# A fused four-layer kernel: the three phase orders of its engines become one order over the whole program

## The chip, the cores and the metric

The kernel runs on one core of a Trainium2 chip. A core has five engines that run side by side and meet at semaphores: PE (TensorE, matrix products and transpositions), DVE (VectorE), ACT (ScalarE), POOL (GpSimd) and SP, which here only issues transfers. The metric is the device time of one launch in microseconds (us); lower is better. The kernel before takes 1239.77 us, the median of three runs (1237.17 to 1240.85).

## The reference

Four layers are applied, one behind the other, to 32 samples of 128 tokens by 128 features; each sample has a condition vector of 128 numbers. All numbers are float32.

```
mod = silu(c) @ W_mod + b_mod                                  # layer 0: 16 heads of 64
x = x + g_msa * attention(modulate(layernorm(x)), W_qkv, W_out)
x = x + g_mlp * ff(modulate(layernorm(x)))                     # ff: 128 -> 512 -> gelu -> 128
x = x + proj(attention(film(rmsnorm(x))))                      # layer 1: one head of 128
x = x + mlp(film(rmsnorm(x)))
x = x + gate1 * attention(modulate(layernorm(x)))              # layer 2: 16 heads of 8
x = x + gate2 * ff(modulate(layernorm(x)))
self = [x, q] @ W_self.T + b_self                              # layer 3: graph attention
for d in range(2):                                             # on A = adj, then adj transposed
    cond, vb = A.sum(-1), A @ w_bias + b_bias                  # adj: 128 x 128 x 11 int32 a sample
    out += gat(self, first 20 tokens as keys, masked by cond > 0, bias vb)
x = x + relu(self + out)
```

## The kernel before

**Groups and streams.** The 32 samples are handled in 8 groups of 4 (`G`, `NG`), so that a tile is 128 partitions by 512 columns. The work of a group is cut into four streams, each a fixed list of steps: the front (layer 0's attention in 8 rounds of two heads, `front_steps`, 77 steps, or 74 for the last group), the middle (layer 0's feed-forward and layer 1, `mid_steps`), the back (layer 2, `back_steps`; it also turns the int32 labels of layer 3 into sums, in 12 pieces, one step of every third) and the end (layer 3, `end_steps`). Below, "front 7" is the front stream of group 7, "end 5" the end stream of group 5, and so on. Names of steps that the text uses: in the front `qk` and `v` (projections), `S` (scores), `T` and `T'` (transposition of the probabilities of one head each), `a` (attention times values), `o` (output projection), `stat`, `unit`, `turn` (norm of the next group: statistics, scaling, transposition and modulation) and `y` (residual); in the back `stat`, `unit`, `turn` of norm 4, then `kq2`, `v2`; in the end `adj` (label sums), `sum3`, `self3`, `qk3` and `u3`, which is thirteen units.

**Four streams at a time.** A stream of a group follows that of the same kind of the group before, and its own group's stream before it. So front g+3, middle g+2, back g+1 and end g run side by side. Every engine has a program of its own, and it is in order: `weave` (line 419) takes one letter after the other from a string and lets the stream of that letter emit its next step on this engine. The strings are tables (`ORDERS`, lines 190 to 244), one for each of PE, DVE, ACT and POOL, in three phases: `head` (fronts 0 to 2, middles 0 and 1, back 0), `steady` (one order of 170 steps, emitted four times, for fronts 3 to 6, middles 2 to 5, backs 1 to 4 and ends 0 to 3) and `tail` (the rest). `order_pairs` (line 256) lists which step must stand before which, and each table is held against it. All loops are Python's, so the built program is straight code.

**PSUM banks.** Results of PE go to 8 banks. `Phase` (line 303) walks PE's order and deals to each result the bank that was released longest ago in that order. It starts anew at each phase. A PE step waits until the bank it writes was emptied by its last reader (`empty`) and until its own inputs are there (`drained`).

**Transfers.** SP's sequence is written out by hand (lines 680 to 712): the input of the next norm (`x_norm`), the residual (`x_res`), the labels of the next group (`adj0`, `adj1`), and the store of a finished group, each behind a wait for the tile's last reader.

## Time and profile before

| | |
|---|---|
| median of three runs | 1239.77 us |
| the profiled execution, whole | 1240.78 us |
| its span, first to last instruction | 1239.0 us |
| PE busy / share | 1110.0 us / 90% |
| DVE busy / share | 879.8 us / 71% |
| ACT busy / share | 772.8 us / 62% |
| POOL busy / share | 434.2 us / 35% |
| mean granted clock of PE | 0.946 |
| instructions | 24134 |

PE is the busiest engine. Steps can be found in the trace, since every step issues a fixed number of instructions of a known line and the engine is in order; so the times of steps below are start times of rows. The four `steady` turns lie between about 308 and 845 us. A granted clock of 1.00 is 2.4 GHz and one of 0.50 is 1.2 GHz. The program before ends with the store of group 7.

### The profile page before, as it was taken

What the parts mean: (1) busy time and instruction counts of PE and PEld (TensorE: products, weight loads), DVE (VectorE), ACT (ScalarE), POOL (GpSimd) and SP (SyncE); (2) the same over time, 40 slices, a digit from 0 to 9 for tenths busy, and PEclk for the clock granted to TensorE, in tenths of its full rate; (3) what the DMA queues carried; (4) which work ended last, traced back from release to release, by engine and by line L of the source; (5) the groups of instructions that cost most, each with busy time, mean ns of one, the idle gap of its engine ahead of it and who ended that gap; (6) DMA issues with size and microseconds to landing.
All of it is one profiled execution on the core that took longest, in us unless ns stands there. A gap on an engine that the chain in (4) does not pass through costs nothing.

```text
span 1239.0 us, 24134 instructions
## 1 busy us (share of the span) xinstructions
PE 1110.0 (90%) x8411; PEld 748.2 (60%) x8411; DVE 879.8 (71%) x2510; ACT 772.8 (62%) x2888; POOL 434.2 (35%) x599
## 2 busy tenths in 40 slices
PE   5889989989999999999999999998989977879865
PEld 4655755665567656775667656765666545646533
DVE  3456656775888688987799688877786478656655
ACT  1646557874688648873787468863866546726622
POOL 1322323332254333541445225432453234214313
PEclk9999999999999999999999999998979998886695
DMA  8000000001000100000000100010000100010000
GB/s 246 2 10 10 10 1 1 10 10 31 1 10 10 31 10 10 1 28 20 9 3 11 39 1 10 2 31 9 10 2 1 38 1 1 1 38 1 1 9 9
DMA packets 21822, 20.98 MB, mean 17 GB/s; under 512 B 1143, under 2 KB 20296, under 8 KB 21448
## 3 DMA queue, kind: packets, MB, share of 16 engines
q1 hardware_dynamic: 18536, 15.26, 4.4%
q10 hardware_dynamic: 3168, 4.19, 1.1%
q8 instruction: 69, 1.13, 0.4%
q14 instruction: 49, 0.40, 0.1%
HBM read 17.35 MB, written 2.10 MB: 16 GB/s over the span
## 4 chain that ended last, share of the span: by engine, by line
PE 63%; DVE 24%; ACT 7%; POOL 3%; issue 2%; DMA 1%; POOLq 0%; DVEq 0%; ACTq 0%
PE bank L1017 9%; PE bank L1036 7%; PE bank L1024 6%; PE bank L1142 5%; PE bank L1041 4%; PE bank L1074 4%; PE bank L1084 4%; PE bank L1150 3%; PE bank L1059 3%; PE bank L1068 3%; PE bank L1011 3%; PE bank L1232 2%; ACT prob_space L947 2%; PE bank L1221 2%; ACT fprobs L883 2%
## 5 line engine op out<-in xcount | busy, mean ns | idle before, releaser
L771 POOL TENSOR_TENSOR fprobs<-fprobs,frinv 128x512 f32<-128x512 f32 x128 | 132.4, 1039 | 282.5 <-DVE frinv L1327 282.2
L883 ACT ACTIVATE fprobs<-bank,fnegmax 128x128 f32<-128x128 f32 x512 | 180.8, 385 | 63.3 <-DVE fnegmax L1322 63.2
L947 ACT ACTIVATE prob_space<-bank,negmax 128x128 f32<-128x128 f32 x512 | 180.7, 380 | 22.2 <-DVE negmax L1451 21.9
L1017 PE MATMUL bank<-fhT,w_qkv 128*128 128x512 f32 x256 | 124.2, 607 | 1.6 <-DVE edge L1521 0.8
L883 ACT ACTIVATION_READ_ACCUMULATOR fprobs<-bank,fnegmax 128x1 f32 x512 | 115.6, 226 | 0.0
L947 ACT ACTIVATION_READ_ACCUMULATOR prob_space<-bank,negmax 128x1 f32 x512 | 113.4, 222 | 0.0
L1322 DVE TENSOR_REDUCE fnegmax<-bank 128x4 f32<-128x512 f32 x128 | 82.1, 682 | 43.7 <-PE bank L1059 43.7
L744 POOL TENSOR_TENSOR rstd<-veps,half 128x4 f32<-128x4 f32 x40 | 40.8, 1019 | 204.5 <-DVE veps L1284 184.3
L1451 DVE TENSOR_REDUCE negmax<-bank 128x4 f32<-128x512 f32 x128 | 82.3, 684 | 31.8 <-PE bank L1142 31.6
L889 ACT ACTIVATE fprobsT<-bank 128x512 f32<-128x512 f32 x128 | 74.4, 602 | 48.6 <-PE bank L1068 48.6
L1150 PE MATMUL bank<-ident,prob_space 128*128 128x128 f32 x512 | 86.3, 300 | 7.6 <-ACT prob_space L947 4.1
L953 ACT ACTIVATE prob_space<-bank 128x512 f32<-128x512 f32 x128 | 76.1, 609 | 26.8 <-PE bank L1150 26.7
L1068 PE MATMUL bank<-ident,fprobs 128*128 128x128 f32 x512 | 75.4, 278 | 17.3 <-POOL fprobs L771 14.8
L1068 PEld LDWEIGHTS bank<-ident,fprobs 128*128 128x128 f32 x512 | 58.7, 142 | 50.2 <-POOL fprobs L771 25.3
L894 ACT ACTIVATE fk<-bank 128x512 f32<-128x512 f32 x64 | 38.6, 603 | 73.2 <-PE bank L1017 72.7
L1142 PE MATMUL bank<-km,qk 32*128 32x256 f32 x512 | 80.9, 437 | 1.0 <-issue 0.8
L1150 PEld LDWEIGHTS bank<-ident,prob_space 128*128 128x128 f32 x512 | 63.4, 153 | 27.9 <-issue 19.8
L1059 PE MATMUL bank<-fk,fq 64*128 64x128 f32 x1024 | 75.2, 287 | 2.2 <-DVE fq L1332 1.6
L1024 PEld LDWEIGHTS bank<-w_qkv,fhT 128*128 128x128 f32 x512 | 64.9, 191 | 18.8 <-issue 16.5
L1059 PEld LDWEIGHTS bank<-fk,fq 64*128 64x128 f32 x1024 | 63.2, 189 | 19.0 <-issue 16.7
L1084 PE MATMUL bank<-fattnT,w_out 128*128 128x512 f32 x128 | 68.5, 617 | 5.6 <-DVE fattnT L1344 5.6
L801 POOL TENSOR_TENSOR adjw<-adjf,labels 80x176 f32<-80x176 f32 (+1 forms) x96 | 54.5, 568 | 52.3 <-ACT adjf L942 52.3
(193 smaller groups left out, 2499.0 us busy)
## 6 DMA issues: line engine op xcount, KB each, us to landing
adj<-in_mask_BxSxSx_ik SPq DMA_DIRECT2D x8, 440.0 KB
adj<-in_mask_BxSxSx_ik SPq DMA_DIRECT2D x32, 110.0 KB
x_norm<-in_x SPq DMA_DIRECT2D x8, 256.0 KB, 2.9
x_res<-in_x SPq DMA_DIRECT2D x8, 256.0 KB, 2.9
out<-x_out SPq DMA_DIRECT2D x8, 256.0 KB, 2.3
w_qkv<-in_L_cond_W_qkv ACTq DMA_DIRECT2D x1, 1536.0 KB, 7.0
prob_space<-in_w_mod SPq DMA_DIRECT2D x1, 1024.0 KB
w_up<-in_w_up ACTq DMA_DIRECT2D x1, 768.0 KB, 12.7
```

The lines of the kernel that those rows point to most:

```text
L771: pool.tensor_tensor(p, p, wide(frinv[:, u, :], D), ALU.mult).then_inc(fnormed.sem, 1)
L883: ins = act.activation(fprobs[:, u % NP, b, :], P.bank(("S", u))[:, tok(b)], ACT.Exp, bias=fnegmax[:, u, b:b + 1], accum_out=frsum[:, u, b ...
L947: ins = act.activation(probs[:, u % NP, i, :], P.bank(("A", u))[:, tok(i)], ACT.Exp, bias=negmax[:, u, i:i + 1], accum_out=rsum[:, u, i:i ...
L1017: ins = pe.matmul(P.bank(result)[:, :], w, a, start=(i == 0), stop=(i == len(terms) - 1))
L1024: ins = pe.matmul(P.bank(result)[:, tok(b)], a[:, tok(b)], w, start=(i == 0), stop=(i == len(terms) - 1))
L1036: pe.matmul(P.bank(result)[:, :], w_up[:, l, tok(c)], part.hT[:, :], start=True, stop=True).then_inc(P.full_sem(result), 1)
L1059: ins = pe.matmul(P.bank(("S", 2 * c + r))[:, tok(b)], fq[rows, c % 2, tok(b)], fk[rows, c % 2, tok(b)], start=True, stop=True)
L1068: ins = pe.transpose(P.bank(("T", u))[:, tok(b)], fprobs[:, u % NP, b, :], ident[:, :])
L1084: ins = pe.matmul(P.bank("o0")[:, :], w_out[:, c, :], fattnT[:, c % 2, :], start=(c == 0), stop=(c == C0 - 1))
L1142: ins = pe.matmul(P.bank(("A", u))[:, tok(2 * n, 2)], qk[strip(u), 0, tok(b)], flat(km[strip(u), b % 2, 2 * n:2 * n + 2, :]), start=True, ...
L1150: ins = pe.transpose(P.bank(("T", u))[:, tok(i)], probs[:, u % NP, i, :], ident[:, :])
L1451: dve.tensor_reduce(negmax[:, u, :], P.bank(("A", u))[:, :].rearrange("p (i k) -> p i k", i=HS), AX.X, ALU.max, negate=True).then_inc(max2 ...
```

## The change

The three phases go. There is one string for each engine over all 1357 steps, with a letter of its own for each stream of each group (fronts A to H, middles I to P, backs Q to X, ends a to h). `Plan` deals the banks once, over the whole of PE's order, in place of `Phase`. The pairs of `order_pairs` are written as a loop over the groups. Two waits are added that the phases had made superfluous: PE waits, before the first `qk` of a front, for the modulated input (`drained("ln0")`), and DVE waits, before the first piece of labels of a back, for its own `bias_ready` of the group before. SP no longer has its sequence written out: its loads and stores are emitted at steps of the streams, in DVE's order.

The strings are not a new arrangement from scratch. Each step's place in PE's order moves by 1.9 places in the mean (at most 17), in DVE's by 1.9 (19), in ACT's by 3.0 (30), in POOL's by 4.1 (49), of 1357. The sequence in which SP issues its transfers is the same, instruction by instruction, and so is the sequence of ACT's 38 table loads, two of exp and gelu in turn.

The diff, cut. Of the strings of letters one line of each side stands:

```diff
@@ -155,19 +155,10 @@
 
 
 
-
-STEPS = {"F": front_steps(), "M": mid_steps(), "B": back_steps(), "E": end_steps(), "A": front_steps(), "Q": front_steps(),
-         "U": mid_steps(), "L": front_steps(False), "N": mid_steps(), "C": back_steps(), "D": back_steps(), "G": end_steps(),
-         "H": end_steps(), "I": end_steps()}
-STEP_NS = {"F": {"qk": 1720, "T": 440, "T'": 440, "S": 1000, "v": 900, "E": 300, "a": 1000, "I": 100, "stat": 300, "unit": 300, "turn": 450,
-                 "o": 860, "y": 500},
...
+for _g in range(NG):
+    STEPS.update({FRONTS[_g]: front_steps(_g + 1 < NG), MIDS[_g]: mid_steps(), BACKS[_g]: back_steps(), ENDS[_g]: end_steps()})
 
 
 NPIECES = 12
...
 ORDERS = {
-    "head": {
+    "all": {
         "PE": (
...
-            "AAAAAAAAAAAAAAAAAAAAAAAAAAAAAAAAAAAAAAAAAAAAAAAAAAAAAAAAAAAAAAAAAAAAAAAAAAAQAQUUQQQQUQQQQQQQQQUQUQQU"
...
+            "IBBBIIBBBBBBBBBIBIBIIBIBIBBBBBBBIBBIBBBIIIBBBBBBBBBBBBIBBBIBIBBIBBIBBCCBBBBCCBBCBCQCCBCCQJJCCCCCJCQC"
...
@@ -261,27 +256,34 @@
 
         pairs.append(((a, len(STEPS[a]) - 1), (b, 0)))
 
-    for f, m in (("Q", "U"), ("F", "M"), ("L", "M")):
-
-        pairs.append((step_at(m, "back", 0), step_at(f, "y")))
-    for a, f in (("A", "Q"), ("Q", "F")):
-
-        pairs += [(step_at(a, x, C0 - 1), step_at(f, y)) for x, y in (("S", "S"), ("I", "E"), ("T'", "T"), ("v", "v"), ("a", "a"), ("o", "o"))]
-        pairs += [(step_at(a, x), step_at(f, y)) for x, y in (("turn", "qk"), ("y", "stat"))]
+    for g in range(NG):
+        f, m, b, e = FRONTS[g], MIDS[g], BACKS[g], ENDS[g]
+
+        follow(f, m)
+        follow(m, b)
+        follow(b, e)
+        if g + 1 == NG:
+            break
+        f2, m2, b2, e2 = FRONTS[g + 1], MIDS[g + 1], BACKS[g + 1], ENDS[g + 1]
+
+        follow(m, m2)
+        follow(b, b2)
+        follow(e, e2)
+
+        pairs.append((step_at(m, "back", 0), step_at(f2, "y")))
+
+        pairs += [(step_at(f, x, C0 - 1), step_at(f2, y)) for x, y in (("S", "S"), ("I", "E"), ("T'", "T"), ("v", "v"), ("a", "a"), ("o", "o"))]
+        pairs += [(step_at(f, x), step_at(f2, y)) for x, y in (("turn", "qk"),)]
+        pairs.append((step_at(f, "y"), step_at(f2, "stat") if g + 2 < NG else step_at(f2, "o", C0 - 1)))
         for c in range(2):
-            pairs += [(step_at(a, "S", C0 - 2 + c), step_at(f, "qk", c)), (step_at(a, "T'", C0 - 2 + c), step_at(f, "S", c)),
-                      (step_at(a, "a", C0 - 2 + c), step_at(f, "T", c)), (step_at(a, "o", C0 - 2 + c), step_at(f, "a", c))]
-        pairs += [(step_at(a, "a", C0 - 4 + c), step_at(f, "v", c)) for c in range(4)]
-
-    for a, b in ("AU", "UM", "QM", "UB", "LN", "MN", "MC", "BC", "ND", "CD", "EG", "BG", "GH", "CH", "HI", "DI"):
-        follow(a, b)
-    for b, m in ("BM", "CN"):
-
-        pairs.append((step_at(b, "y2"), step_at(m, "down", (1, 1))))
-    for e, b in ("EB", "GC", "HD"):
-
-        pairs.append((step_at(e, "adj"), (b, EDGE_EVERY * 3)))
-        pairs.append((step_at(e, "u3", NU3 + 4), step_at(b, "down", (2, 1))))
+            pairs += [(step_at(f, "S", C0 - 2 + c), step_at(f2, "qk", c)), (step_at(f, "T'", C0 - 2 + c), step_at(f2, "S", c)),
+                      (step_at(f, "a", C0 - 2 + c), step_at(f2, "T", c)), (step_at(f, "o", C0 - 2 + c), step_at(f2, "a", c))]
+        pairs += [(step_at(f, "a", C0 - 4 + c), step_at(f2, "v", c)) for c in range(4)]
+
+        pairs.append((step_at(b, "y2"), step_at(m2, "down", (1, 1))))
+
+        pairs.append((step_at(e, "adj"), (b2, EDGE_EVERY * 3)))
+        pairs.append((step_at(e, "u3", NU3 + 4), step_at(b2, "down", (2, 1))))
     return pairs
 
 
...
@@ -300,57 +302,51 @@
         assert not order_faults(_order), (_name, order_faults(_order))
 
 
-class Phase:
-
-
-
-    def __init__(self, banks, orders, turns=1, prefer=range(8)):
+class Plan:
+
+
+
+    def __init__(self, banks, orders, prefer):
         self.banks, self.orders = banks, orders
         order = orders["PE"]
-        self.base = list(banks.dealt)
         starts = {x: [p for p, y in enumerate(order) if y == x] for x in set(order)}
         ends = {(x, r): starts[x][i] for x in starts for i, s in enumerate(STEPS[x]) for r in s.ends}
         free_from = {b: i - 100 for i, b in enumerate(prefer)}
-        for _ in range(2 if turns > 1 else 1):
-            self.at, self.per = {}, [0] * 8
-            went = dict.fromkeys(starts, 0)
-            for p, x in enumerate(order):
-                for r in STEPS[x][went[x]].begins:
-                    b = min(free_from, key=lambda b: free_from[b])
-                    assert free_from[b] < p, (p, x, r)
-                    free_from[b] = ends[x, r]
-                    self.at[x, r] = (b, self.per[b])
-                    self.per[b] += 1
-                went[x] += 1
-            free_from = {b: p - 1000 for b, p in free_from.items()}
-        for b in range(8):
-            banks.dealt[b] += turns * self.per[b]
-
-    def view(self, letter, turn):
-        return View(self, letter, turn)
+        self.at, dealt = {}, [0] * 8
+        went = dict.fromkeys(starts, 0)
+        for p, x in enumerate(order):
+            for r in STEPS[x][went[x]].begins:
+                b = min(free_from, key=lambda b: free_from[b])
+                assert free_from[b] < p, (p, x, r)
...
@@ -642,6 +632,14 @@
         def strip(u):
             return slice(32 * (u % S4), 32 * (u % S4) + 32)
 
+        def run(name, prologue, front, mid, back, last):
+            prologue()
+            streams = {}
+            for letters, stream in ((FRONTS, front), (MIDS, mid), (BACKS, back), (ENDS, last)):
+                streams.update({letter: stream(plan.view(letter), g) for g, letter in enumerate(letters)})
+
+            weave(plan.orders["DVE" if name == "SP" else name], streams)
+
...
-            for g in range(2):
-                sp.wait_ge(*fz_ready.nth(g, 0))
-                load_norm(g + 1)
-            for g, mid_letter in enumerate("UM"):
-                sp.wait_ge(*head.view(mid_letter, 0).drained("z0"))
-                load_res(g + 1)
-                sp.wait_ge(*fz_ready.nth(g + 2, 0))
-                load_norm(g + 3)
-            sp.wait_ge(*adj_summed.nth(0, NPIECES - 1))
-            load_edges(1)
-
-            def steady_loads(it, norm):
-                sp.wait_ge(*steady.view("M", it).drained("z0"))
-                load_res(it + 3)
-                if norm is not None:
-                    sp.wait_ge(*fz_ready.nth(it + 4, 0))
-                    load_norm(norm)
-                sp.wait_ge(*adj_summed.nth(it + 1, NPIECES - 1))
-                load_edges(it + 2)
-                store(steady.view("E", it), it)
-
-            for it in range(NG - 4):
-                steady_loads(it, it + 5 if it + 5 < NG else None)
-            sp.wait_ge(*tail.view("M", 0).drained("z0"))
-            load_res(NG - 1)
-            sp.wait_ge(*adj_summed.nth(NG - 3, NPIECES - 1))
-            load_edges(NG - 2)
-            store(tail.view("E", 0), NG - 4)
-            sp.wait_ge(*adj_summed.nth(NG - 2, NPIECES - 1))
-            load_edges(NG - 1)
-            for i, letter in enumerate("GHI"):
-                store(tail.view(letter, 0), NG - 3 + i)
+            sp.wait_ge(*fz_ready.nth(0, 0))
+            load_norm(1)
+
+            def front(P, g):
+                for what, _, _, _ in STEPS[P.letter]:
+                    if what == "unit" and g + 2 < NG:
+                        sp.wait_ge(*fz_ready.nth(g + 1, 0))
+                        load_norm(g + 2)
+                    yield
+
+            def mid(P, g):
+                for what, _, _, _ in STEPS[P.letter]:
+                    if what == "back" and g + 1 < NG:
+                        sp.wait_ge(*P.drained("z0"))
+                        load_res(g + 1)
+                    yield
+
+            def back(P, g):
+                for i in range(len(STEPS[P.letter])):
+                    if i == EDGE_LAST and g + 1 < NG:
+                        sp.wait_ge(*adj_summed.nth(g, NPIECES - 1))
+                        load_edges(g + 1)
+                    yield
+
+            def last(P, g):
+                for what, _, _, _ in STEPS[P.letter]:
+                    if what == "y3":
+                        store(P, g)
+                    yield
+
+            run("SP", lambda: None, front, mid, back, last)
...
-
-        def run(name, prologue, front, mid, back, last):
-            prologue()
-            weave(head.orders[name], A=front(head.view("A", 0), 0), Q=front(head.view("Q", 0), 1), F=front(head.view("F", 0), 2),
-                  U=mid(head.view("U", 0), 0), M=mid(head.view("M", 0), 1), B=back(head.view("B", 0), 0))
-            for it in range(NG - 4):
-                weave(steady.orders[name], F=front(steady.view("F", it), it + 3), M=mid(steady.view("M", it), it + 2),
-                      B=back(steady.view("B", it), it + 1), E=last(steady.view("E", it), it))
-            weave(tail.orders[name], L=front(tail.view("L", 0), NG - 1), M=mid(tail.view("M", 0), NG - 2),
-                  N=mid(tail.view("N", 0), NG - 1), B=back(tail.view("B", 0), NG - 3), C=back(tail.view("C", 0), NG - 2),
-                  D=back(tail.view("D", 0), NG - 1), E=last(tail.view("E", 0), NG - 4), G=last(tail.view("G", 0), NG - 3),
-                  H=last(tail.view("H", 0), NG - 2), I=last(tail.view("I", 0), NG - 1))
 
         @block.gpsimd
         def _(pool):
@@ -1045,12 +1030,15 @@
             def front(P, g):
                 for what, c, _, _ in STEPS[P.letter]:
                     if what == "qk":
+                        if c == 0 and g:
+
+                            pe.wait_ge(*plan.view(FRONTS[g - 1]).drained("ln0"))
                         linear(P, f"q_{c}", [(w_qkv[:, tok(c)], fhT[:, :])])
                         linear(P, f"k_{c}", [(w_qkv[:, tok(C0 + c)], fhT[:, :])])
                     elif what == "v":
...
@@ -1440,6 +1428,9 @@
                     if not 0 <= p < NPIECES:
                         return
                     d, e0, n = PIECES[p]
+                    if p == 0 and g:
+
+                        dve.wait_ge(*bias_ready.nth(g - 1, 0))
                     dst = edge1[:, :, e0:e0 + n] if d else edge0[:, :, 0, e0:e0 + n]
                     dve.wait_ge(*adjw_ready.nth(g, p))
                     _, labels, weighted = edge_views(p)
@@ -1495,7 +1486,7 @@
                         add(P, "y2", x, x1)
                     elif what == "down" and k == (2, 1):
                         dve.wait_ge(*P.drained("xt"))
-                        if P.phase is not head:
+                        if g:
 
                             dve.wait_ge(*rel_ready.nth(g - 1, 1))
                         dve.wait_ge(*P.full("g2"))
```

Three places show what the strings do. The names are those of the profile: `fattnT` is what `o` reads, `fz` the gated result that `y` transposes, `x3T` the input of layer 3, `z` and `mz` the scaled norms of the back and of the middle, `hT` and `mhT` the modulated ones, `edge` the label sums. Line numbers after the change are lower by 8 to 15.

PE before, at the end of front 7, from the last but one `o` on:

```order
L1084 MATMUL bank<-fattnT,w_out 128x512
L1074 MATMUL bank<-fprobsT,fv 64x128 x8
L1084 MATMUL bank<-fattnT,w_out 128x512
L1011 MATMUL bank<-ident,fz 128x128 x4
L1182 MATMUL bank<-ident,edge 128x80 x2
L1017 MATMUL bank<-x3T,ones 128x512
L1011 MATMUL bank<-ident,z 128x128 x4
L1017 MATMUL bank<-x3T,w 128x512
L1017 MATMUL bank<-q,w 128x512
L1017 MATMUL bank<-hT,w_l 128x512 x2
```

PE after, the same place:

```order
L1072 MATMUL bank<-fattnT,w_out 128x512
L1062 MATMUL bank<-fprobsT,fv 64x128 x8
L1002 MATMUL bank<-x3T,ones 128x512
L1072 MATMUL bank<-fattnT,w_out 128x512
L996 MATMUL bank<-ident,z 128x128 x4
L1002 MATMUL bank<-x3T,w 128x512
L1002 MATMUL bank<-q,w 128x512
L996 MATMUL bank<-ident,fz 128x128 x4
L1002 MATMUL bank<-hT,w_l 128x512 x2
```

The transposition of back 6 (`ident,z`) and the first products of end 5 (`x3T`) now stand ahead of front 7's last step (`ident,fz`), and the label sums (`edge`) further up.

DVE before, at the same place, from the copy behind the last but one `a` on:

```order
L1344 COPY fattnT<-bank 128x512
L1356 COPY fmod<-mod 128x4
L1344 COPY fattnT<-bank 128x512
L1302 TENSOR_SCALAR fz<-bank,col,fmod 128x128 x4
L1364 TENSOR_TENSOR x_res<-bank,x_res 128x512
L1398 COPY gmod<-mod 128x64
L1459 TENSOR_SCALAR biasg<-gmod,col 128x4
L1272 BN_STATS stats<-x 128x6 x4
L1275 MEMSET held 128x1
L1277 BN_AGGR mv<-stats 128x2 x4
L1284 TENSOR_SCALAR veps<-mv 128x4
L1518 COPY gcond<-condT 128x4
```

DVE after:

```order
L1332 COPY fattnT<-bank 128x512
L1386 COPY gmod<-mod 128x64
L1450 TENSOR_SCALAR biasg<-gmod,col 128x4
L1260 BN_STATS stats<-x 128x6 x4
L1263 MEMSET held 128x1
L1265 BN_AGGR mv<-stats 128x2 x4
L1272 TENSOR_SCALAR veps<-mv 128x4
L1344 COPY fmod<-mod 128x4
L1332 COPY fattnT<-bank 128x512
L1528 TENSOR_SCALAR q<-bank,gcond 128x128 x4
L1280 TENSOR_SCALAR z<-x,mv,rstd 128x128 x4
L1290 TENSOR_SCALAR fz<-bank,col,fmod 128x128 x4
```

The statistics of back 6 stand between two copies of front 7, where DVE waited for PE, and its scaling (`z`) ahead of `fz`.

PE before, around norm 2 of middle 7 (`mz`), with bank numbers and waits:

```order
L1232 MATMUL bank6<-kbd,q3 128x80 [waits bank7_free,bank6_free]
L1232 MATMUL bank7<-kbd,q3 128x80
...
L1150 MATMUL bank4<-ident,prob_space 128x128 [waits bank4_free,bank1_free]
L1150 MATMUL bank4<-ident,prob_space 128x128 x3
L1150 MATMUL bank3<-ident,prob_space 128x128 [waits bank3_free,bank2_free]
L1150 MATMUL bank3<-ident,prob_space 128x128 x3
L1011 MATMUL bank7<-ident,mz 128x128 [waits bank7_free,mid_z_ready]
```

PE after:

```order
L1130 MATMUL bank5<-km,qk 128x256 [waits bank6_free,bank5_free,km_ready]
L1130 MATMUL bank6<-km,qk 128x256
...
L1138 MATMUL bank7<-ident,prob_space 128x128 [waits bank7_free,bank5_free]
L1138 MATMUL bank7<-ident,prob_space 128x128 x3
L1138 MATMUL bank1<-ident,prob_space 128x128 [waits bank1_free,bank6_free]
L1138 MATMUL bank1<-ident,prob_space 128x128 x3
L996 MATMUL bank6<-ident,mz 128x128 [waits bank6_free,mid_z_ready]
```

The transposition stands at the same place, but its bank was last held by scores of back 6, which ACT reads, and no longer by scores of end 5, which DVE reads at unit 3.

## Rows read from the trace of the kernel before

**Rows 1.** The page: span, busy time of each engine with its share.
```profile
span 1239.0 us, 24134 instructions
PE 1110.0 (90%) x8411; PEld 748.2 (60%) x8411; DVE 879.8 (71%) x2510; ACT 772.8 (62%) x2888; POOL 434.2 (35%) x599
```
**Rows 2.** Busy time by stretch: length, PE, PEld, DVE, ACT, POOL, clock, DMA.
```profile
165.00:308.00 143.00, 128.97 (x956) 85.65 (x954) 92.05 (x281) 92.87 (x358) 41.17 (x48) 0.99 0.04 11
845.00:920.00 75.00, 66.75 (x437) 43.72 (x437) 58.95 (x161) 49.45 (x192) 32.86 (x48) 0.86 0.02 5
1032.00:1083.00 51.00, 42.66 (x361) 30.80 (x361) 36.29 (x101) 34.67 (x126) 20.21 (x29) 0.80 0.01 1
1083.00:1239.00 156.00, 116.60 (x742) 75.88 (x742) 91.32 (x249) 64.47 (x215) 48.05 (x80) 0.73 0.04 12
```
**Rows 3.** Busy time in the third steady turn, same columns.
```profile
569.70:704.30 134.60, 129.68 (x1054) 87.96 (x1050) 110.05 (x313) 94.99 (x360) 53.43 (x73) 1.00 0.05 14
```
**Rows 4.** PE's waits in that turn: for whom, us, times, longest.
```profile
PE bank L1017 <- DVE edge L1521: 1.2, 1, 1.2
PE bank L1011 <- DVE z L1292: 0.8, 1, 0.8
```
**Rows 5.** Busy time in stretches of half clock, columns of rows 2.
```profile
903.40:917.10 13.70, 12.46 (x83) 9.57 (x84) 10.96 (x27) 6.25 (x25) 9.13 (x11) 0.50 0.00 1
1033.10:1043.30 10.20, 9.37 (x36) 5.68 (x37) 8.40 (x19) 4.50 (x21) 6.34 (x8) 0.50 0.00 0
1121.90:1162.90 41.00, 39.05 (x251) 27.68 (x247) 24.79 (x61) 28.85 (x127) 14.52 (x25) 0.50 0.01 1
```
**Rows 6.** Timeline around 990 to 1003: start, us, instruction, [idle before, releaser].
```profile
989.40 0.69 DVE L1344 COPY fattnT<-bank 128x512 f32<-128x512 f32 x1 [2.18 <-PE bank L1074]
991.38 1.37 DVE L1302 TENSOR_SCALAR fz<-bank,col,fmod 128x128 f32<-128x128 f32 x4 [1.29 <-PE bank L1084]
997.75 1.11 DVE L1292 TENSOR_SCALAR z<-x,mv,rstd 128x128 f32<-128x128 f32 x4
998.77 1.12 DVE L1537 TENSOR_SCALAR q<-bank,gcond 128x128 f32<-128x128 f32 x4
998.91 1.09 PE L1011 MATMUL bank<-ident,z 128*128 128x128 f32 x4 [4.41 <-DVE z L1292]
1002.96 1.45 PE L1017 MATMUL bank<-hT,w_l 128*128 128x512 f32 x3
```
**Rows 7.** Timeline from 851 to 857.
```profile
852.71 1.28 DVE L1322 TENSOR_REDUCE fnegmax<-bank 128x4 f32<-128x512 f32 x2
856.35 3.78 PE L1017 MATMUL bank<-hT,w_l 128*128 128x512 f32 x4 [2.84 <-DVE hT L1297]
```
**Rows 8.** Timeline from 1031 to 1034.
```profile
1031.31 0.86 DVE L1290 TENSOR_SCALAR mz<-mx,rstd 128x128 f32<-128x128 f32 x4
1033.35 0.43 DVE L1570 TENSOR_TENSOR p<-bank,keep 128x320 f32<-128x320 f32 x1
1033.93 1.09 PE L1011 MATMUL bank<-ident,mz 128*128 128x128 f32 x4 [3.93 <-DVE p L1570]
```
**Rows 9.** Timeline of PE from 79 to 98.
```profile
79.93 0.66 PE L1068 MATMUL bank<-ident,fprobs 128*128 128x128 f32 x4 [1.56 <-POOL fprobs L771]
88.57 1.88 PE L1017 MATMUL bank<-fhT,w_qkv 128*128 128x512 f32 x4
90.76 1.06 PE L1024 MATMUL bank<-w_qkv,fhT 128*128 128x128 f32 x8
97.54 0.85 PE L1011 MATMUL bank<-ident,mz 128*128 128x128 f32 x4 [1.82 <-DVE mz L1292]
```
**Rows 10.** PE's waits from 165 to 308, columns of rows 4.
```profile
PE bank L1084 <- DVE fattnT L1344: 2.4, 3, 0.8
PE bank L1068 <- ACT fk L894: 1.5, 1, 1.5
```
**Rows 11.** All waits of the span: DVE's only one for a load.
```profile
DVE stats L1272 <- DMA x_norm<-in_x: 8.6, 1, 8.6
```

156 lines of the change are left out of this document (77 added, 79 removed).

## The prediction

> **What bounds the kernel.** I read the page first: of a span of 1239.0 us PE is busy 1110.0, DVE 879.8 [rows 1]. The change adds and removes no work, so what can move is PE's waiting (129.0 us) and its clock. Then busy time by stretch [rows 2], to see where the waits lie: 14.0 us of 143 from 165 to 308, 8.3 of 75 from 845 to 920, 8.3 of 51 from 1032 to 1083, 39.4 of 156 behind 1083. A steady turn instead lasts 134.6 us and has 129.7 of PE in it at full clock [rows 3]: 4.9 us of waits, four times. So the turns are near PE's work, and the stretches in which the phases meet are looser: at the turn's rate (3.7%) the three named first would hold 9.8 us of waits and not 30.6. Last the granted clock: 0.86, 0.80 and 0.73 in the stretches from 845 on, 1.00 in the turn [rows 2, 3]. In half-clock stretches PE is busy nearly throughout (12.5 of 13.7 us, 9.4 of 10.2, 39.1 of 41.0 [rows 5]); of such busy time half is what the clock costs, since two projections take 1.88 us at full clock and 3.78 at half [rows 7, 9].
>
> **The change, place by place.** Times are of the profiled execution: its span 1239.0 and 1.8 around it, 1240.8, which is 1.0 above the median of 1239.8; I take that 1.0 off in the end.
>
> A. End of front 7. From the copy behind the last `a` (989.40) to back 6's `kq2` (1002.96) pass 13.6 us [rows 6]. DVE waits 1.29 us for `o`, gates `fz`, and only then takes the statistics of back 6, the label tiles and `z`, for which PE waits 4.41. After, statistics and labels stand ahead of the copy, in DVE's former waits (2.18 in rows 6), and from the copy on DVE has copy 0.69, `q` 1.12, `z` 1.11, `fz` 1.37 and `hT`, which has the shape of `fz`, 1.37: 5.7 in a row. On PE `q` needs `sum3` first, so that `z` is done at about 3.3; behind it stand the transposition (0.66), `self3`'s two products (1.88) and `y` (0.66), so `kq2` starts at about 6.5, when `hT` is there too. Gain 13.6 - 6.5 = 7.1, full clock assumed.
>
> B. Start of back 5. PE waits 2.84 us for `hT` before `kq2` [rows 7]. After, DVE modulates directly behind front 7's row maxima, and `adj` and `v` (1.06 [rows 9]) stand ahead of `kq2` on PE. Behind `z` DVE has a residual add of 0.7, the maxima 1.28 and the modulation 1.37, 3.3 together; PE has a transposition 0.66, `adj` 0.3 and `v` 1.1, so about 1.2 of waiting is left: gain 1.6 here and 0.8 just ahead, 2.4. `kq2` ran at half clock; that costs 1.9 by its 3.78, and some 3.0 with what follows it. I take half: 3.9 in all, between 1 and 5.4.
>
> C. 893 to 917. PE waits for POOL and DVE at end 4's units (8.3 us in 845 to 920, less the 3.7 of B, 4.6), and the clock falls at 903.4 for 13.7 us [rows 2, 5]. The new order puts one transposition (0.66) more ahead of the waiting unit, little else. Between 0 and 4.6 + 6.2; I take 2.0, near the 0.66 and a part of the clock.
>
> D. Middle 7's norm 2. `mz` is ready at 1032.17, but PE starts at 1033.93, when DVE has read unit 3's scores out of bank 7 [rows 8]. After, the bank is one that ACT empties earlier: 1.8 of the 3.9 go. Then the clock falls for 10.2 us, with PE busy 9.4 [rows 5]; half of it, 4.7, would come back if it didn't, and I take half of that, 2.3. Further down `u3` and transpositions move ahead of waits of 1 to 2 us, 1.0 taken. 5.1, between 1 and 16 (all 8.3 of the stretch and more clock).
>
> E. End of front 0. Front 1's `qk` and `v`, 1.88 + 1.06, move ahead of `T`, which waits 1.56 and then 0.7 [rows 9]. But the same 1.88 lay between `o` and `y` before, and covered the gate (1.37): that wait opens. What remains is 0.9, and `qk` ahead of the `mz` transposition covers 0.4 more of its 1.82. With half of the half-clock stretch behind it 2.1, between 0.5 and 3.
>
> F. 165 to 308. `qk`, `S` and `v` now stand before both `o` of front 1 (its share of the 2.4 us is 1.6) and two steps before the `T'` that waited 1.5 [rows 10]; with `y` and the clock behind the second 4.0 of 14.0, between 0 and 8.
>
> S. The four turns. `kq2` waits 1.2 us for a bank that holds the label sums, and the `z` transposition before it 0.8 [rows 4]. After, middle g+2's scaling (1.1) is no longer ahead of `z` on DVE, in all turns. Of 8.2 us I take 3.0. The bounds are -8 and +33 (below).
>
> G. Behind 1083. PE's order moves by two places at most here, and the waits are those of one chain: 0, between -6 and +6.
>
> H. What the moves open elsewhere. Nearly every step moves by a place or two. A turn, one tuned order, has seven waits of 0.7 in the mean (4.9 in all). I put two more of them into each 134.6 us from 77 to 1083: 7.5 x 1.4 = +10.5. It may be 0, or twice that.
>
> Sum: 7.1 + 3.9 + 2.0 + 5.1 + 2.1 + 4.0 + 3.0 = 27.2, less 10.5, is 16.7. 1240.8 - 16.7 - 1.0 = 1223.1: **1223 us**.
>
> The other edits cost nothing. PE's new wait for the modulated input stands five or more of PE's working steps behind the transposition that feeds it, against one modulation of 1.4 us. DVE's is for a result of its own, earlier in its order. SP issues the same transfers in the same order. The one load that any engine waits for is the first [rows 11], which doesn't move; were SP's loads later by some us, they would still be hidden.
>
> **A rule against the sum.** The sum holds that a turn can win its waits and no more, since PE's busy time is a floor: in the third turn PE is busy 129.7 of 134.6 us [rows 3]. The Trainium skill, page "Perfetto Trace Analysis", section "Identifying the Most-Contended Engine", says that matmul busy time is no good measure of nearness to the roofline, and the weight loads' is. By it the turn would not be bound by PE: weight loads are busy 88.0 us of it, DVE 110.1 [rows 3]. The turn could then fall until DVE binds, by up to 24.5 us, four times 98: about 1125. Against it in rows: between waits PE's instructions stand end to start, and a reordering changes none of them; so far the trace does not bear the rule out.
>
> **Rivals.**
> 1. The clock stays up. If the waits at 903 and 1033 shrink, the half-clock stretches behind them may go whole: 6.2 more in C, 2.4 in D and about 4 in the two further dips to 1071, and H is 3 rather than 10.5. 1223 - 12.6 - 7.5 = 1203. For it: each dip sits behind a wait of over 1.5 us. Against: waits of 1.2 and 1.8 in one stretch may do as well.
> 2. Given back. The named waits go, but the end is one chain from end 6 to the store, in which the clock is half for 41 us [rows 5] anyway. If that stretch grows by the 25 us that are at full clock around it, PE's work there takes 12 more: 1223 + 12, and a few us of H: 1236 to 1243.
> 3. Slower, through banks in the turns. The new plan deals other banks in each turn, and a step can meet one whose reader is late, as bank 7 did for 1.8 us [rows 8]. If the turns wait like 165 to 308 does (9.8% in place of 3.7%), each is 8.2 longer, 33 in four, against 24.2 won elsewhere: 1240 + 9 = 1249. It decides from about 6 us a turn on, three or four such meetings. For it: before's turn was one order, tuned and repeated; now four different ones. Against: the distance from a bank's release to its next use, in PE's order, is the same before and after (three steps or more, seven mostly).
> 4. The rule above, 1125.
> That the change does nothing is half true: SP's sequence is unchanged, so all of the effect must come from the four strings.
>
> **How the numbers follow.** Forecast (1212 to 1235) 0.52; rival 1 (1195 to 1212) 0.17; rival 2 0.15; rival 3 0.15; rival 4 0.01. About 0.3%, 3.7 us, is what a measurement can tell from no change. Faster: 0.52 + 0.17 + 0.01 = 0.70; same, rival 2, 0.15; slower 0.15. The range reaches into rival 1 and over most of rival 2: 1206 to 1241. The forecast's own is 1212 to 1235.
>
> **What would show it.** A: from the copy behind the last `a` of front 7 to `kq2` of back 6 under 8 us. B: the wait before back 5's `kq2` near 1.2. D: the transposition of middle 7's `mz` within 0.3 us of `mz`. E: a new wait of 1.4 before front 0's `y`, none of 1.56 at its last `T`. S: turns of about 134. H: waits that before doesn't have, some 10 us. PE's busy time in the turns unchanged. I am wrong if a turn is over 137 or under 130, if the clock from 845 to 1083 is 1.00 throughout (rival 1), or if the part behind back 7's start grows by over 6 us (rival 2).

## The result and the profile after

The changed kernel takes **1183.87 us** (median of 4 runs, 1181.46 to 1187.39) against 1240.31 of before beside it (1237.17 to 1244.25): ratio 0.9546, interval 0.9509 to 0.9582. Faster by 56 us; 1223 was forecast, with a range from 1206.

The page of after, answering to [rows 1]; the execution took 1181.46 us.

```profile
span 1179.7 us, 24111 instructions
PE 1085.0 (92%) x8411; PEld 734.9 (62%) x8411; DVE 881.7 (75%) x2510; ACT 770.1 (65%) x2888; POOL 435.8 (37%) x599
```

Two things moved. PE waits 94.7 us (1179.7 - 1085.0) and not 129.0: 34.3 less. And PE's busy time, with the same 8411 matmuls, is 25.0 shorter: less of it at half clock. To see where, I cut after at the PE steps at which the prediction's windows begin and end. A cut falls behind the same number of steps, not always behind the same steps. First the stretches of before that no group has shown (columns of rows 2):

```profile
0.00:165.00 165.00, 139.27 (x969) 95.98 (x971) 87.95 (x252) 85.69 (x321) 45.02 (x54) 0.99 0.17 52
308.00:845.00 537.00, 516.91 (x4179) 351.08 (x4178) 438.81 (x1244) 379.56 (x1440) 212.75 (x291) 1.00 0.05 14
920.00:1032.00 112.00, 98.80 (x777) 65.07 (x777) 74.45 (x227) 66.07 (x243) 34.18 (x49) 0.98 0.04 12
```

and all seven of after, with its third turn last, answering to [rows 2, 3]:

```profile
0.00:163.40 163.40, 141.43 (x965) 97.45 (x966) 88.56 (x253) 86.70 (x327) 45.83 (x55) 0.99 0.18 53
163.40:292.90 129.50, 127.01 (x977) 85.40 (x975) 93.52 (x292) 92.76 (x351) 41.25 (x49) 1.00 0.04 12
292.90:822.10 529.20, 520.15 (x4175) 354.91 (x4176) 439.47 (x1238) 378.05 (x1440) 214.07 (x291) 0.99 0.05 14
822.10:889.60 67.50, 60.09 (x416) 39.66 (x416) 56.56 (x149) 48.63 (x191) 29.47 (x45) 0.92 0.02 5
889.60:993.90 104.30, 97.30 (x787) 65.37 (x789) 78.29 (x236) 66.75 (x246) 36.73 (x52) 1.00 0.04 12
993.90:1035.60 41.70, 33.88 (x363) 24.64 (x362) 36.46 (x104) 33.00 (x122) 21.52 (x29) 1.00 0.01 2
1035.60:1179.70 144.10, 105.14 (x739) 67.43 (x736) 88.81 (x242) 64.21 (x216) 46.91 (x79) 0.79 0.05 13
550.90:681.40 130.50, 128.70 (x1047) 88.76 (x1046) 109.26 (x314) 95.22 (x361) 54.22 (x73) 1.00 0.05 14
```

Length less PE is the waiting. Side by side, in us:

| stretch of before | length | waits | PE busy | forecast of the length |
|---|---|---|---|---|
| 0-165 | -1.6 | 25.7 to 22.0 | +2.2 | E -2.1 |
| 165-308 | -13.5 | 14.0 to 2.5 | -2.0 | F -4.0 |
| 308-845 (turns) | -7.8 | 20.1 to 9.1 | +3.2 | S -3.0, most of H +10.5 |
| 845-920 | -7.5 | 8.3 to 7.4 | -6.7 | B, C -5.9 |
| 920-1032 | -7.7 | 13.2 to 7.0 | -1.5 | A -7.1 |
| 1032-1083 | -9.3 | 8.3 to 7.8 | -8.8 | D -5.1 |
| behind 1083 | -11.9 | 39.4 to 39.0 | -11.5 | G 0 |

Down to the end of the turns the gain is waits (26.3 of 34.3), in the last phase it is mostly clock (28.4 less PE busy behind 845 of before). Two rows need a second look. In 0-165 PE is 2.2 us busier: the profiled execution of after ran its first projections at half speed, that of before did not, and neither did that of `s2_head` (experiment 2), which has the same new order there. The first four products in before, after and `s2_head`, in this order:

```profile
22.81 1.98 PE L1017 MATMUL bank<-fhT,w_qkv 128*128 128x512 f32 x4 [0.56 <-DVE fhT L1297]
```
```profile
22.63 3.78 PE L1002 MATMUL bank<-fhT,w_qkv 128*128 128x512 f32 x4 [0.55 <-DVE fhT L1285]
```
```profile
22.58 1.98 PE L1002 MATMUL bank<-fhT,w_qkv 128*128 128x512 f32 x4 [0.56 <-DVE fhT L1285]
```

`s2_head` takes 160.6 us for this stretch, so the order gained 4.4 here and not 1.6. And in 845-920 after has 416 matmuls for before's 437. Time at half clock went from about 20.5 us to 10.2, worth some 4.5; about 2 us of the 7.5 are work that only lies on the other side of a cut, so B, C gave about 5.

The places that the prediction worked out came as it said. Timeline of PE (with one row of DVE in it) where it answers to [rows 6 to 9]:

```profile
93.52 1.11 PE L996 MATMUL bank<-ident,fz 128*128 128x128 f32 x4 [1.54 <-DVE fz L1290]
102.69 0.66 PE L996 MATMUL bank<-ident,mz 128*128 128x128 f32 x4 [1.44 <-DVE mz L1280]
...
825.13 1.13 PE L1002 MATMUL bank<-hT,w_l 128*128 128x512 f32 x2 [1.38 <-DVE hT L1285]
...
957.05 0.69 DVE L1332 COPY fattnT<-bank 128x512 f32<-128x512 f32 x1 [0.42 <-PE bank L1062]
960.30 0.66 PE L996 MATMUL bank<-ident,z 128*128 128x128 f32 x4 [1.38 <-DVE z L1280]
962.95 1.89 PE L1002 MATMUL bank<-hT,w_l 128*128 128x512 f32 x4
...
993.04 0.66 PE L996 MATMUL bank<-ident,mz 128*128 128x128 f32 x4 [1.19 <-DVE mz L1278]
```

B: 1.38 us of waiting before back 5's `kq2`, where 2.84 were and 1.2 was forecast. A: from the copy to `kq2` 5.9 us (962.95 - 957.05), where 13.6 were and 6.5 was forecast. D: PE takes `mz` at once, not after the reader of bank 7. E: the wait for the gate has opened (1.54; forecast 1.4). The waits from 163.4 to 292.9 answer to [rows 10]; the two largest:

```profile
PE bank L1056 <- POOL fprobs L756: 1.1, 2, 0.6
PE bank L996 <- DVE mz L1280: 0.3, 1, 0.3
```

### The profile page after: what moved, and what is told of

It is laid out like the page before. It is cut to its first block, busy times and chain, and to the rows that moved or that the text cites. A ratio compares the mean times of both kernels' runs of the same rounds, so it can differ in the third digit from the quotient of the medians.

```text
span 1179.7 us, 24111 instructions
## 1 busy us (share of the span) xinstructions
PE 1085.0 (92%) x8411; PEld 734.9 (62%) x8411; DVE 881.7 (75%) x2510; ACT 770.1 (65%) x2888; POOL 435.8 (37%) x599
## 4 chain that ended last, share of the span: by engine, by line
PE 68%; DVE 19%; ACT 5%; POOL 4%; issue 3%; DMA 1%; POOLq 0%; DVEq 0%; ACTq 0%
PE bank L1002 11%; PE bank L1021 7%; PE bank L1009 7%; PE bank L1026 5%; PE bank L1047 5%; PE bank L1072 5%; PE bank L1062 5%; PE bank L1056 4%; PE bank L1130 4%; PE bank L1138 3%; PE bank L996 3%; PE bank L1148 2%; PE bank L1220 2%; PE bank L1209 2%; ACT prob_space L932 2%
## 5 line engine op out<-in xcount | busy, mean ns | idle before, releaser
L1138 PE MATMUL bank<-ident,prob_space 128*128 128x128 f32 x512 | 78.6, 287 | 6.0 <-ACT prob_space L932 5.6
L1130 PE MATMUL bank<-km,qk 32*128 32x256 f32 x512 | 75.6, 422 | 3.5 <-POOL km L793 2.2
L1138 PEld LDWEIGHTS bank<-ident,prob_space 128*128 128x128 f32 x512 | 60.6, 147 | 27.3 <-issue 17.6
L838 POOL TENSOR_TENSOR p<-p,rinv 128x320 f32<-128x320 f32 x64 | 47.3, 740 | 75.8 <-DVE rinv L1548 75.8
## 6 DMA issues: line engine op xcount, KB each, us to landing
w_up<-in_w_up ACTq DMA_DIRECT2D x1, 768.0 KB, 13.2
```

The costliest lines, as they stand in the source:

```text
L1130: ins = pe.matmul(P.bank(("A", u))[:, tok(2 * n, 2)], qk[strip(u), 0, tok(b)], flat(km[strip(u), b % 2, 2 * n:2 * n + 2, :]), start=True, ...
L1138: ins = pe.transpose(P.bank(("T", u))[:, tok(i)], probs[:, u % NP, i, :], ident[:, :])
```

## Experiments

All were timed beside before, whose median was 1241.43 in the first four, 1242.66 in the next four, 1241.32 and 1240.86 in the last two sets. Most cut before's and after's strings at a step and join them, in the form of the changed kernel (one string, letters A to X and a to h). Of such an edit one line of a string stands; the others differ likewise.

**1. The form alone.** `s1_one_plan`: before's phases laid end to end in one string, one plan of banks, SP's transfers emitted from the steps. Cut from the changed kernel:

```diff
...
-            "AAAAAAAAAAAAAAAAAAAAAAAAAAAAAAAAAAAAAAAAAAAAAAAAAAAAAAAAAAAAAAAAAAABBAAAAAAAAAIBIBBBBBIBBBBBBIBBIBBI"
+            "AAAAAAAAAAAAAAAAAAAAAAAAAAAAAAAAAAAAAAAAAAAAAAAAAAAAAAAAAAAAAAAAAAAAAAAAAAABABIIBBBBIBBBBBBBBBIBIBBI"
...
```

> The changed code, but the strings hold the old three phases' orders, laid end to end: one bank plan, the two added waits and SP's woven sequence without any move of a step. Theory 1 (all of the effect is in the moved steps): 1240, within 4 us of before. Theory 2 (a good part comes from dealing the banks without a fresh start at each phase): 1215 to 1230.

Measured 1242.79, ratio 1.0018 (0.9996 to 1.0039). The new form is worth nothing that can be told from zero; all lies in the strings.

**2. Phase by phase.** `s2_head`, `s3_turns`, `s4_tail`: the new strings in the first phase, in the four turns, or in the last phase only, against `s1_one_plan`. A line of each:

```diff
...
-            "AAAAAAAAAAAAAAAAAAAAAAAAAAAAAAAAAAAAAAAAAAAAAAAAAAAAAAAAAAAAAAAAAAAAAAAAAAABABIIBBBBIBBBBBBBBBIBIBBI"
+            "AAAAAAAAAAAAAAAAAAAAAAAAAAAAAAAAAAAAAAAAAAAAAAAAAAAAAAAAAAAAAAAAAAABBAAAAAAAAAIBIBBBBBIBBBBBBIBBIBBI"
...
```

> As one_plan, with the new order inside the first phase alone (fronts 0 to 2, middles 0 and 1, back 0), the rest in the old order. Theory 1 (the gain is local and additive; by the two traces PE has done the first 329 steps 17 us earlier): 1220 to 1226. Theory 2 (moving the head only shifts when later waits and clock falls come, so that little of it is kept): 1232 to 1240.

```diff
...
-            "GGUGUGdUdVVHeOHHHHHHHVeOOVHVHVeVVVOeVOeVVHVOVHHHVOHeHVHVHeOHVHOHVVVVeHHVVeeVOVOVeVVeOHVHeOHHHOHVHeHV"
+            "GNUGUUUdGVVHeOHHHHHHHVeOOVHVHVeVVVOeVOeVVHVOVHHHVOHeHVHVHeOHVHOHVVVVeHHVVeeVOVOVeVVeOHVHeOHHHOHVHeHV"
...
```

> As one_plan, with the new order inside the four steady turns alone. Theory 1: the two traces give 6.5 us here, with one fall of the clock in the new one: 1228 to 1236. Theory 2 (turns tuned one by one are no better than one repeated turn, and the 6.5 us come from what was before): 1238 to 1244.

```diff
...
-            "PfWWfPWWWPWWPPWWfPWWPWPfPWfWPWWPWWPfPWWWfWWfWWPWPffWWfWPWPWWWWPPWfWWWWgXXXgXXXgXXggXXXXgXXgXXXXXXXXg"
+            "WPWWWPPPWWfWWPWWfWPfWPWPfWWfWPPWPWWWPWWfWWPfWWPfPWWWfWfWPWPWWfWPWPWWWWgXXXgXXXXXgXgXXXXgXgXXXXgXXXXX"
...
```

> As one_plan, with the new order inside the last phase alone (front 7 on). Theory 1: the two traces give 35 us from PE step 1009 on: 1203 to 1209. Theory 2 (a part of the tail's gain is the clock, which falls by chance of when a wait comes, so it is not tied to these moves): 1212 to 1225.

Measured 1223.16 (ratio 0.9844, 0.9797 to 0.9891), 1233.56 (0.9936, 0.9918 to 0.9955) and 1211.96 (0.9773, 0.9741 to 0.9806): by these ratios 19, 8 and 28 us, 55 of the 56. The first two fall where their expectation had them. The third is 3 us above its theory 1 and just outside theory 2 (from 1212), so it decides between neither.

**3. The seams.** `s5_seams`: new strings, but no step ahead of one of an earlier phase. From it to the changed kernel:

```diff
...
-            "DaRDDKRKDDDaDKRRDRKRRKDDKRDDDRaDDKDDDRDDDaRKDDKDRRKDDDKDRDRDKDRDaRDDDaDRDKRDKDDDDRKaRDDRRaKRDRDaRRaE"
+            "DaRDDKRKDDDaDKRRDRKRRKDDKRDDDRaDDKDDDRDDDaRKDDKDRRKDDDKDRDRDKDRDaRDDDaDRDKRDKDDDDRKaRDDRRaKRDRDaRREa"
...
```

> The changed kernel with its new order inside every phase, but with the seams kept: no step of one phase stands ahead of a step of an earlier one (8 of PE's 1357 steps, 12 of VectorE's, 29 of ScalarE's and 70 of GpSimd's go back for that). Theory 1, the gain lies in the order inside the phases (the three phases alone gave 19, 8 and 28 us): 1184 to 1190 us. Theory 2, moving steps across the seams, which only one order for the whole program allows, gives a part of it: over 1192 us.

Measured 1187.54, ratio 0.9555 (0.9532 to 0.9577), 3.7 us above the changed kernel by the medians and 1 us by the ratios to before: theory 1. Moving steps across the seams, the thing that only one order allows, is a small part, and the intervals don't tell it from nothing.

**4. What in the last phase.** `s6_tail_a` has the new order to PE's step 1215 (about 1036 us of before), `s7_tail_b` from there on.

```diff
...
-            "PfWWfPWWWPWWPPWWfPWWPWPfPWfWPWWPWWPfPWWWfWWfWWPWPffWWfWPWPWWWWPPWfWWWWgXXXgXXXgXXggXXXXgXXgXXXXXXXXg"
+            "WPWWWPPPWWfWWPWWfPWWPWPfPWfWPWWPWWPfPWWWfWWfWWPWPffWWfWPWPWWWWPPWfWWWWgXXXgXXXgXXggXXXXgXXgXXXXXXXXg"
...
```

> The new order only from the start of the last phase to PE's step 1215 (before: 1009 to 1037 us, turns of fronts, middle and back 5 and 6), the order of before ahead of it and behind it. In the trace of before and after this stretch holds 11 us of the last phase's 28, and 17 lie behind it. Theory 1, what is gained behind step 1215 (TensorE 28 us less at half clock there) is a consequence of the waits closed ahead of it, and comes with them: 1212 to 1218 us, and the stretch behind 1215 is as long as in the changed kernel. Theory 2, it comes from the order behind 1215 itself: 1226 to 1233 us.

```diff
...
-            "PfWWfPWWWPWWPPWWfPWWPWPfPWfWPWWPWWPfPWWWfWWfWWPWPffWWfWPWPWWWWPPWfWWWWgXXXgXXXgXXggXXXXgXXgXXXXXXXXg"
+            "PfWWfPWWWPWWPPWWfWPfWPWPfWWfWPPWPWWWPWWfWWPfWWPfPWWWfWfWPWPWWfWPWPWWWWgXXXgXXXXXgXgXXXXgXgXXXXgXXXXX"
...
```

> The new order only from PE's step 1215 to the end, the order of before ahead of it. Theory 1 (the gain behind 1215 follows from what stands ahead of it): 1238 to 1242 us. Theory 2 (it comes from the order there): 1221 to 1228 us, with less time at half clock behind step 1215.

Measured 1224.01 (0.9856, 0.9819 to 0.9894) and 1229.91 (0.9900, 0.9878 to 0.9922): 18.6 and 12.8 us, which add up to the phase's 28 and 3 more, and neither theory's figure. Behind 1083 of before, the windows of `s1_one_plan`, `s6_tail_a` and `s7_tail_b` (columns of rows 2):

```profile
1083.90:1243.00 159.10, 120.96 (x742) 78.10 (x742) 91.03 (x249) 64.57 (x215) 48.12 (x80) 0.70 0.04 11
```
```profile
1064.60:1221.90 157.30, 119.15 (x742) 77.47 (x742) 91.50 (x249) 64.47 (x215) 47.87 (x80) 0.71 0.04 12
```
```profile
1079.60:1228.50 148.90, 110.25 (x739) 70.82 (x736) 88.13 (x242) 64.32 (x216) 46.90 (x79) 0.73 0.05 12
```

The waits are 38.1, 38.2 and 38.7. With the order of before there, the stretch takes 156.0 to 159.1 us and PE is busy 116.6 to 121.0 in six kernels (before, `s1_one_plan`, `s2_head`, `s6_tail_a`, `s12_bank`, `s13_place_a`), whatever stood ahead; with the new one 144.1 to 149.0 and 105.1 to 110.3 in the changed kernel, `s4_tail` and `s7_tail_b`. So it is the new order there, which I had priced at nothing, that lets the same work run with less of it at half clock. It explains 7 to 10 us of the 11.9: before's 156.0 is the shortest of the one kind and the changed kernel's 144.1 the shortest of the other, and the 4.8 us between that and `s7_tail_b` no run assigns. From there on up to 1083, from before's 1034, `s6_tail_a` gains some 3 us more in an unchanged order. (Two numbers of the expectations don't come out of the traces: behind step 1215 after has some 40 us less at half clock than before, not 28, and the gain in an unchanged order is this 3, not 4.4.)

**5. Whose order.** Behind step 1215 the new order on DVE, ACT and POOL but not on PE (`s18_tail_b_others`, edit against `s7_tail_b`), and in the first phase on PE and DVE but not on ACT and POOL (`s15_head_pe_dve`, against `s2_head`).

```diff
...
-            "PfWWfPWWWPWWPPWWfWPfWPWPfWWfWPPWPWWWPWWfWWPfWWPfPWWWfWfWPWPWWfWPWPWWWWgXXXgXXXXXgXgXXXXgXgXXXXgXXXXX"
+            "PfWWfPWWWPWWPPWWfPWWPWPfPWfWPWWPWWPfPWWWfWWfWWPWPffWWfWPWPWWWWPPWfWWWWgXXXgXXXgXXggXXXXgXXgXXXXXXXXg"
...
```

> Behind PE's step 1215 the new order on VectorE, ScalarE and GpSimd, and the order of before on PE; ahead of it the order of before. With PE's new order too it was 1229.9 us. Theory 1, PE's moves of one or two places there matter little and the other engines' order closes the waits: 1228 to 1233 us. Theory 2, PE's places do it: 1238 to 1243 us.

```diff
...
-            "CJCQCQCCCCCQQQCCCQCQQJQJCCCCCKRDaDDaRKKDDaaDRDRRDDaRDRRRKKRRDDDRDRDKDRKDRDRKaDDRDRDDKKDaDaRRRDDDDDDK"
+            "CQCCCQCCCCCJQCCCCQCQCCQQCCQQQKRDaDDaRKKDDaaDRDRRDDaRDRRRKKRRDDDRDRDKDRKDRDRKaDDRDRDDKKDaDaRRRDDDDDDK"
...
```

> The new order in the first phase on PE and VectorE alone; ScalarE and GpSimd keep the order of before there, and everything behind the phase is as before. The new order on all four gave 1223.2 us. Theory 1, PE's and VectorE's order closes the waits (my terms E and F, which I read from these two): 1222 to 1228 us. Theory 2, the larger moves of ScalarE and GpSimd (up to 23 places) do it, since half of the waits there are for exponentials and probabilities: 1232 to 1242 us.

Measured 1245.93 (1.0059, 1.0034 to 1.0085) and 1233.55 (0.9968, 0.9935 to 1.0000). Theory 2 in the second; the first is slower still than its theory 2 (1238 to 1243). Three engines in the new order and PE in the old one are 5 us slower than before, and 16 slower than with PE moved along; behind 1083 the stretch then takes 156.1 us, with 42.1 of waits, for `s7_tail_b`'s 148.9. With ACT and POOL left behind the head gives 7 of its 19 us. Where F lay, 143.0 us of before, the new order on all four engines takes 129.1 (`s2_head`) and on PE and DVE alone 141.2 (columns of rows 2):

```profile
160.60:289.70 129.10, 125.41 (x959) 84.03 (x959) 90.81 (x280) 91.48 (x351) 40.34 (x48) 1.00 0.04 12
```
```profile
164.70:305.90 141.20, 130.32 (x959) 86.04 (x959) 92.33 (x280) 92.61 (x351) 40.36 (x48) 0.98 0.04 11
```

The largest waits of the latter:

```profile
PE bank L1130 <- ACT mhid L898: 2.2, 1, 2.2
PE bank L1056 <- POOL fprobs L756: 1.9, 4, 0.6
PE bank L996 <- DVE fz L1290: 1.5, 1, 1.5
PE bank L1009 <- ACT mhid L893: 1.3, 1, 1.3
```

Two of the four are for ACT at work on `mhid`, in ACT's old order; in after neither is there. The waits for `fprobs`, the largest of before's, shrank with PE's and DVE's order alone:

```profile
PE bank L1068 <- POOL fprobs L771: 5.1, 6, 1.8
```

Other mixes of engines over the whole program were not tried.

**6. Moves at random.** Neighbouring steps of different streams exchanged, 45 pairs in before (`s10_rand45`), 30 in after (`s16_rand_after`): all of them on PE, and on each other engine the 17 to 29 that stood in the same order there.

```diff
...
-            "CCCQJCQJQQJJQQQQCCQCQQCJCQCCCCCCQJQQJCQQCQJQCCQQCCCCQJQQCJJCCJCQCQJQCJQCCCJQQJCCQQQJCQQCCQCQCJCCCCQJ"
+            "CCCQJCQJQQJJQQQQCCQCQQCJCQCCCCCCQJQQJCQQCQJQCCQQCCCQCJQQCJJCCJCQCQJQCJQCCCJQQJCCQQQJCQQCCQCQCJCCCCQJ"
...
```

> The order of before with 45 pairs of neighbouring steps of different streams exchanged, drawn at random, on all four engines alike; nothing is chosen by time. The prediction held that moved steps open new waits of their own (its term H, 10.5 us for 1000 moved steps, a tenth of which move here). Theory 1, moves at random open waits at about that rate or above it: 1242 to 1250 us. Theory 2, PE is so rarely short of input that neighbours can be exchanged freely: within 2 us of before, 1238 to 1242 us.

```diff
...
-            "bEEEEELEEESEbLSESLLESEEESSSEbELEESbLEEEEEEESLLSESbESSEbLELESEbSESESSFbTTMFFFcTMFcTTFFMFcFFTcTTMcMTTT"
+            "SEEEEELEEESEbLSESLLESEEESSSEbELEESbLEEEEEEESLLSESbESSEbLELESEbSESESSFbTTMFFFcTMFcTTFFMFcFFTcTTMcMTTT"
...
```

> The changed kernel with 30 pairs of neighbouring steps of different streams exchanged on all engines alike, drawn at random: 19 in the turns, 9 in the last phase. Theory 1, the turns stay within 1 us each and the last phase gets longer by some us, as 16 random exchanges in it did to the order of before (13.6 us): 1187 to 1197 us. Theory 2, the new order has so few waits that exchanges are free: 1182 to 1186 us.

Measured 1254.04 (1.0098, 1.0056 to 1.0139) and 1196.11 (0.9671, 0.9621 to 0.9722): 12 us lost each time. The second is within its theory 1, the first above it (1242 to 1250). Where: the turns of `s10_rand45` (28 of its exchanges, seven places four times over) and then 920 to 1083 of before.

```profile
307.50:842.80 535.30, 515.71 (x4179) 351.60 (x4176) 437.12 (x1244) 380.17 (x1440) 212.53 (x292) 1.00 0.05 14
919.20:1094.80 175.60, 143.75 (x1139) 95.96 (x1138) 111.95 (x328) 100.31 (x367) 54.77 (x79) 0.89 0.03 8
```

The turns take 535.3, not more than the 537.0 of before. The other stretch takes 175.6, where before's takes 163.0, with 31.9 us of waits for 21.5 and the clock at 0.89 for 0.93. In `s16_rand_after` 8.6 of the 13.0 us by which its profiled execution is longer than the changed kernel's lie behind the turns. So moves that nobody chose cost in the last phase, and there more than H: 45 exchanges, a tenth of the change's moved steps, took 12 us, and H charged 10.5 for all of them. In the turns they cost nothing. The change's moves opened fewer waits than they closed in every stretch: they are not of the kind that I had priced.

**7. One order for all turns.** `s11_turn4`: the changed kernel with the order of its fourth turn in the other three.

```diff
...
-            "cFFMTFFMFcTFMTMcTTcTFFFFMFcTMTFFTFTFTTGUGcUGGGGdGdUGNUUGNdUNUdUUNNdUdNUUUUGGNGdUUGGGNUGGGNGUGGNGUGUG"
+            "MFcTFFFFMcTFFFMMTFFcTcTTFFMcTFFMTFTTTGUcGFUGGGGdGdUGNUUGNdUNUdUUNNdUdNUUUUGGNGdUUGGGNUGGGNGUGGNGUGUG"
...
```

> The changed kernel with the order of its fourth turn in all four turns (its own turns last 133.0, 137.0, 130.6 and 131.9 us; the second holds 10.2 us at half clock). Theory 1, a stretch's time belongs to its order and is repeated with it: three turns of 131.8 in place of 133.0, 137.0 and 130.6, 5 us less than the changed kernel, 1177 to 1182 us. Theory 2, each turn's order is fitted to the banks and streams that its neighbours leave it: 1184 to 1192 us.

Measured 1185.78, ratio 0.9568 (0.9523 to 0.9613): no gain, theory 2. Two of its turns:

```profile
548.80:681.60 132.80, 130.41 (x1047) 88.05 (x1046) 111.08 (x312) 94.10 (x360) 54.00 (x73) 1.00 0.05 14
681.60:815.30 133.70, 131.31 (x1049) 88.43 (x1048) 111.08 (x312) 94.10 (x360) 54.00 (x73) 1.00 0.05 12
```

Each waits 2.4 us. The second is the fourth turn, whose string is unchanged; in the changed kernel it waits 1.4:

```profile
686.50:818.40 131.90, 130.47 (x1052) 88.48 (x1051) 111.19 (x316) 94.48 (x361) 54.02 (x73) 1.00 0.04 12
```

So what stands ahead of a turn changes its waits, here by 1 us. The gain that theory 1 expected did not come.

**8. Single places.** `s12_bank`: before with another bank for middle 7's norm 2. `s13_place_a`: before with the new order between steps 1150 and 1200 only. `s14_place_a_old`: after with before's order between 1160 and 1190.

```diff
...
+                if (x, r) == ("P", "ln2"):
+                    b = sorted(free_from, key=lambda b: free_from[b])[1]
...
```

> The order of before throughout, with one thing altered: the transposition of middle 7's norm 2 is dealt the second longest free bank in place of bank 7 (and what is dealt behind it follows). PE waits 1.8 us there for the reader of bank 7, and then the clock falls for 10.2 us. Theory 1 (my term D): the 1.8 go and half of what the clock costs there, 2.3, so 1236 to 1239 us. Theory 2, the wait alone goes: 1239 to 1241 us. Theory 3, the clock stays up behind it through the further stretches to 1163, 32 us of them at a cost of about 0.43 us each: under 1230 us.

```diff
...
-            "PfWWfPWWWPWWPPWWfPWWPWPfPWfWPWWPWWPfPWWWfWWfWWPWPffWWfWPWPWWWWPPWfWWWWgXXXgXXXgXXggXXXXgXXgXXXXXXXXg"
+            "WPWWfPWWWPWWPPWWfPWWPWPfPWfWPWWPWWPfPWWWfWWfWWPWPffWWfWPWPWWWWPPWfWWWWgXXXgXXXgXXggXXXXgXXgXXXXXXXXg"
...
```

> The new order only between PE's steps 1150 and 1200 (end of front 7, back 6's norm, kq2 and first end steps), the order of before elsewhere. Term A gave 7.1 us for this place; between before and after its two stretches (PE's steps 1111 to 1185) differ by 10.2 us. Theory 1, the place gives what it gives and nothing behind it: 1231 to 1235 us. Theory 2, with its waits gone the clock behind it stays up as in the run with the new order to step 1215 (4.4 us less in steps 1241 to 1270 with the same order): 1224 to 1229 us.

```diff
...
-            "HVHHeHOVHVHHHHVeVOHHOHVeHVVeHOVOHHHVHHOHHHVHVVOOeHHHHVVOVHHVHHHOHVVHHfWHHHHHfWHWfHWWfPWPWWPffPPWWWfP"
+            "HVHHeHOVHVHHHHVeVOHHOHVeHVVeHOVOHHHVHHOHHHVHVVOOeHHHHVVOVHHVHVVHHHOHHHHWHHHHHWffWfWWfPWPWPWffPPWWWfP"
...
```

> The changed kernel with the order of before between PE's steps 1160 and 1190, so that PE waits for z ahead of back 6's kq2 again (4.4 us before). Theory 1, the place costs its own 7 to 10 us: 1190 to 1195 us. Theory 2, the wait also brings the clock down further on (the changed kernel has none at half clock in steps 1111 to 1270): over 1197 us.

Measured 1236.00 (0.9966, 0.9927 to 1.0005; 1225.88 to 1241.26 in ten runs), 1236.60 (0.9967, 0.9945 to 0.9990) and 1188.98, which is 5 us above the changed kernel. The first median lies where theory 1 had it, but its interval reaches over no change at all, and the trace doesn't bear that theory out: in `s12_bank` PE's wait before `mz` goes from 3.93 to 2.25 [rows 8], and the half clock comes all the same (0.65 over the next 14.8 us); then what lies behind takes 157.3 us, as elsewhere in the old order (156.0 to 159.1):

```profile
1028.40 0.66 PE L998 MATMUL bank<-ident,mz 128*128 128x128 f32 x4 [2.25 <-DVE mz L1280]
```
```profile
1028.20:1043.00 14.80, 13.40 (x75) 9.35 (x79) 13.60 (x30) 8.94 (x37) 8.24 (x11) 0.65 0.00 1
1077.60:1234.90 157.30, 119.22 (x742) 77.47 (x742) 90.98 (x249) 64.48 (x215) 48.08 (x80) 0.70 0.04 12
```

`s13_place_a` came out 1.6 us above theory 1's range (1231 to 1235). In it `kq2` of back 6 comes 5.9 us behind the copy, as in after, 920 to 1032 takes 106.8 us for 112.0, and nothing is won behind it: 1032 to 1083 takes 51.3, with the clock at 0.77.

```profile
918.00:1024.80 106.80, 96.74 (x777) 64.26 (x777) 74.79 (x229) 66.57 (x245) 34.16 (x49) 1.00 0.04 12
1024.80:1076.10 51.30, 43.29 (x361) 31.73 (x361) 36.29 (x100) 34.22 (x124) 20.15 (x29) 0.77 0.01 1
```

`s14_place_a_old` is the same place from the other side. Its 5 us are a little under theory 1's 7 to 10; in its trace the stretch takes 112.1 us for the changed kernel's 104.3:

```profile
884.80:996.90 112.10, 101.81 (x787) 67.50 (x789) 79.01 (x237) 67.37 (x248) 36.83 (x52) 0.97 0.04 12
```

**9. Waits of known length.** `s17_delay`, against the changed kernel:

```diff
...
+        idle = sb("idle", [D, G, D])
...
+        idled = count("idled", 1)
...
+                for n in range({2: 2, 3: 4, 4: 8}.get(g, 0) if k == 4 else 0):
+                    normalize(part.stat, idle, src, k).then_inc(idled.sem, 1)
+                    dve.wait_ge(idled.sem, {2: 1, 3: 3, 4: 7}[g] + n)
                 normalize(part.stat, part.z, src, k).then_inc(part.z_ready.sem, 1)
...
```

> The changed kernel in which VectorE normalizes back 2, back 3 and back 4 (in turns 2, 3 and 4) two, four and eight times more into an unused tile before it does so for use: 2.3, 4.6 and 9.2 us of added work ahead of a transposition that PE takes soon after. Theory 1, a wait of some two microseconds brings the clock to half for 7 to 14 us behind it: each of the three delays is followed by such a stretch, and the time is 1184 + 10 to 16 of waiting + 9 to 15 for the clock, 1203 to 1215 us. Theory 2, one wait in busy surroundings leaves the clock alone, whatever its length: no new stretch at half clock in turns 3 and 4, 1192 to 1200 us.

Measured 1201.73, ratio 0.9718 (0.9663 to 0.9772), 18 us above the changed kernel. PE's waits at the three places, and the two stretches at half clock in the turns:

```profile
423.17 0.66 PE L998 MATMUL bank<-ident,z 128*128 128x128 f32 x4 [1.35 <-DVE z L1282]
...
559.33 1.12 PE L998 MATMUL bank<-ident,z 128*128 128x128 f32 x4 [4.60 <-DVE z L1282]
...
700.79 1.12 PE L998 MATMUL bank<-ident,z 128*128 128x128 f32 x4 [7.37 <-DVE z L1282]
```
```profile
558.30:565.10 6.80, 5.78 (x16) 3.97 (x17) 6.61 (x22) 1.51 (x8) 0.00 (x0) 0.50 0.00 0
698.20:705.00 6.80, 4.21 (x8) 2.04 (x9) 6.62 (x27) 2.90 (x16) 1.01 (x1) 0.50 0.00 0
```

A wait of 1.35 us left the clock at full, waits of 4.60 and 7.37 each brought it down for 6.8, and the fall began while PE was still waiting (558.3 and 698.2, before 559.33 and 700.79). The time is a little under theory 1's 1203; its "each of the three" failed for the shortest.

## Why the prediction was wrong

**What held.** A: 5.9 us where 6.5 was forecast, length -7.7 for -7.1, and -5.2 when that place alone is changed. B's wait is as forecast, and B and C together gave about 5 for 5.9. The new wait at E is there, though the stretch gained 4.4 for 2.1. D's mechanism is there: PE waits for `mz` and not for a bank. In the third turn PE is busy 128.7 us, 129.7 before, so the floor of the sum held. The kernel's form cost nothing, as the prediction said of the other edits.

The Trainium skill, page "Perfetto Trace Analysis", section "Identifying the Most-Contended Engine", calls matmul busy time no good measure of nearness to the roofline and takes the share of peak arithmetic and the weight loads' busy share instead. Read as a forecast, as rival 4 did, it didn't come true here: weight loads are busy 88.8 us of a turn of 130.5, DVE 109.3, and the turn stayed at PE's matmul time. How near that is to the chip's roofline no run here measured.

**Where it failed**, in the order of size:

- **G, 0 against 11.9.** "PE's order moves by two places at most here" misread the strings: in the line of PE's string shown in experiment 2 for `s4_tail`, end 6's fifth step (the fifth `g`) comes five places later and its seventh four. The waits did stay (39.4 to 39.0). But PE's busy time there is 11.5 us shorter, at a clock of 0.79 for 0.73. The step that failed is the one from "same waits" to "same time": it left out where the half clock falls. `s7_tail_b` showed that the order there gives 7 to 10 us of it, `s18_tail_b_others` that PE's moves are needed for it.
- **H, +10.5 against nothing.** I charged a rate for moves without a choice behind them. Random exchanges do cost 12 us, with a tenth of the moved steps, but no stretch of after waits longer than before, and the turns' 20.1 us of waits became 9.1.
- **F, 4.0 against 13.5.** Mis-sized: its upper bound was 8, by two steps that I could name. All but 2.5 of the stretch's 14.0 us of waits went, also most of those for `fprobs` (5.1 to 1.1), which F had not named. `s15_head_pe_dve` showed what was left out: PE's and DVE's strings alone, from which I had worked, give 1.8 of the 13.9 us that all four give in this stretch, and 7 of 19 in the whole head.
- **S, 3.0 against 7.8**: waits -11.0, PE busy +3.2, with a dip of the clock in the second turn, of which below. Two waits were named, more closed.
- **D, 5.1 against 9.3.** The wait's share did not come (8.3 to 7.8 in the stretch: other waits took its place), the clock came whole (0.80 to 1.00). With 1.7 us of the wait before `mz` away and 2.25 left the half clock still came (`s12_bank`); with 1.19 left, in after, it did not. Whether the length of that wait decides it is not shown: the whole order differs between the two.

That makes 11.9 + 10.5 + 9.5 + 4.8 + 4.2 = 40.9 of the 42.6 us by which the profiled execution (1181.5) fell short of its forecast (1240.8 - 16.7 = 1224.1). The rest is A, B, C and E. Rival 1 was on the right side, with the clock at 1.00 from 993.9 to 1035.6, but 845 to 920 kept dips (0.92) and it knew nothing of the head and the end; rivals 2 and 3 were wrong.

**What stays open.** That waits bring the clock down is shown by `s17_delay`, for waits of over 4 us. Why about the same sum of waits behind 1083 leaves PE 105 to 110 us of work in one order and 117 to 121 in the other is not shown by any row, nor is why `s6_tail_a` gains some 3 us behind its last moved step. Which single moves close the head's waits was not tried.

## What to carry over

Read a reordering on every engine, not on the one that waits: without the strings of ACT and POOL the head gave less than half of its gain, and at the end the new order on three engines without PE's lost time. Price the waits of a whole stretch down to what a well-ordered stretch of the same kernel has (165 to 308 went from 9.8% of waits to 1.9%, below the turns' 3.7%), not only those that a named move explains, and charge for new waits where nobody chose the moves. And where the clock is below 1, keep waits and clock apart in the sum: three of seven stretches got shorter with their waits nearly unchanged. Before a difference of a few us in one stretch is put down to an order, look at the same order in a second kernel: here the first projections, one turn and the end each differed by 3 to 5 us between profiles with the same order.

## What the runs showed of the hardware

The clock differs between executions of one order. The second turn of after fell to half clock behind a wait of 2.21 us; with the same order of that turn, in `s14_place_a_old`, it did not, behind the same wait. The wait in each, and the windows of the two:

```profile
433.87 1.55 PE L1130 MATMUL bank<-km,qk 32*128 32x256 f32 x8 [2.21 <-POOL km L793]
```
```profile
433.57 1.13 PE L1130 MATMUL bank<-km,qk 32*128 32x256 f32 x8 [2.21 <-POOL km L793]
```

```profile
419.00:556.00 137.00, 133.23 (x1049) 91.06 (x1048) 113.14 (x314) 94.79 (x360) 51.89 (x72) 0.96 0.05 14
```
```profile
418.70:550.80 132.10, 128.33 (x1048) 88.07 (x1047) 112.24 (x313) 94.66 (x360) 52.16 (x72) 1.00 0.05 14
```

In these windows PE waits 3.8 us both times; the first is at half clock for 10.2 us and 4.9 us longer, so a microsecond at half clock cost 0.48 here. Four runs of after differ by 5.9 us (1179.7 to 1185.6 of span) with the granted clock going from 0.965 to 0.955, and ten of `s12_bank` by 15 us. A stretch at full clock, by contrast, repeats: before's turn takes 134.5 to 134.7 us in ten kernels that keep it, with the old head or the new one ahead of it. Where the turn ahead changes, it can differ (experiment 7).
